# Attention with relative positions and a mixture of experts on one core: preparing the next pair's operands in other rounds and on other engines

## The reference

```python
x = x + attention(layernorm(x)); x = x + experts(layernorm(x))
# attention:
Q, K, V = x @ Wq.T + bq, x @ Wk.T + bk, x @ Wv.T + bv          # 16 heads of 8
rel_pos = arange(L)[None, :] - arange(L)[:, None] + 127        # rows of relative_k, relative_v; clipped
scores = einsum('bhld,bhrd->bhlr', Q, K) / sqrt(8) + einsum('bhld,lrd->bhlr', Q, relative_k[rel_pos])
attn = softmax(scores)
out = einsum('bhlr,bhrd->bhld', attn, V) + einsum('bhlr,lrd->bhld', attn, relative_v[rel_pos])
return out @ Wo.T + bo
```

## Time and profile before

| what | value |
|---|---|
| median of 3 runs | 2184.48 us (2182.93 to 2188.32) |
| profiled execution, its own time | 2185.62 us |
| its span | 2183.6 us |
| mean granted TensorE clock | 0.992 |
| TensorE busy | 2092.8 us, 96% of the span |
| VectorE busy | 1704.3 us, 78% |
| ScalarE busy | 1502.6 us, 69% |
| GpSimd busy | 1059.9 us, 49% |

### The profile page before, as it was taken

The page is one execution under the profiler, slowest core; times in us unless marked ns, Lnnn a source line. Parts: engine busy times, 40 slices in busy tenths (PEclk is TensorE's granted clock), DMA queues, the critical chain, the costliest instruction groups (busy, mean ns, idle before and its releaser), DMA issues.

```text
span 2183.6 us, 88119 instructions
## 1 busy us (share of the span) xinstructions
PE 2092.8 (96%) x37442; PEld 1546.1 (71%) x37442; DVE 1704.3 (78%) x3959; ACT 1502.6 (69%) x3290; POOL 1059.9 (49%) x992
## 2 busy tenths in 40 slices
PE   3999999999999999999999999999998999999998
PEld 2776777777677767777776777677776777777776
DVE  4888888888788888888887888888875666667675
ACT  3666676666666666766666666666665888888887
POOL 2444343344344443443443444434423777777676
PEclk8999999999999999999999999999999999999999
DMA  5112211321221122113212211222112112212210
GB/s 137 41 45 66 73 54 44 84 64 54 65 73 52 46 65 72 54 45 84 63 54 65 73 50 47 65 63 64 44 54 32 27 23 24 27 21 24 29 20 11
DMA packets 255679, 114.46 MB, mean 52 GB/s; under 512 B 142218, under 2 KB 251156, under 8 KB 255348
## 3 DMA queue, kind: packets, MB, share of 16 engines
q1 hardware_dynamic: 255348, 109.60, 20.4%
HBM read 83.34 MB, written 8.39 MB: 42 GB/s over the span
## 4 chain that ended last, share of the span: by engine, by line
PE 74%; DVE 9%; ACT 7%; issue 4%; POOL 3%; SPq 1%; DMA 1%; ACTq 0%; POOLq 0%; DVEq 0%
PE ps L1253 17%; PE ps L1186 10%; PE ps L1273 9%; PE ps L1283 7%; PE ps L1193 7%; PE ps L1204 6%; POOL probs_t L498 3%; DVE probs_t L791 2%; ACT probs L643 2%; ACT probs L576 2%; PE ps L1434 2%; PE ps L1417 2%; PE ps L1419 2%; PE ps L1418 2%; PE ps L1435 2%
## 5 line engine op out<-in xcount | busy, mean ns | idle before, releaser
L576 ACT ACTIVATE probs<-ps,neg_max 128x512 f32<-128x512 f32 x1024 | 690.4, 686 | 396.0 <-DVE neg_max L786 396.0
L786 DVE TENSOR_REDUCE neg_max<-ps 128x1 f32<-128x512 f32 x1024 | 635.5, 683 | 123.6 <-PE ps L1193 120.9
L437 POOL TENSOR_TENSOR stat_hi<-q_twice,mask8h 128x1024 f16<-128x1024 f16 x128 | 243.8, 1904 | 851.6 <-PE ps L1193 739.2
L1253 PE MATMUL ps<-const,probs 128*128 128x128 f32 x4096 | 506.1, 275 | 21.5 <-DVE probs_t L791 20.2
L1253 PEld LDWEIGHTS ps<-const,probs 128*128 128x128 f32 x4096 | 454.0, 142 | 62.4 <-issue 26.8
L791 DVE COPY probs_t<-ps 128x512 f32<-128x512 f32 x512 | 339.3, 682 | 91.4 <-PE ps L1253 89.5
L498 POOL TENSOR_TENSOR probs_t<-probs,probs_t 128x1024 f16<-128x1024 f32 x160 | 340.0, 2133 | 109.3 <-ACT probs_t L649 109.3
L566 ACT ACTIVATE probs_t<-ps 128x512 f32<-128x512 f32 x512 | 283.9, 596 | 149.1 <-PE ps L1253 145.0
L1186 PE MATMUL ps<-keys,stat_hi 128*32 128x512 f16 x4096 | 318.0, 383 | 0.0
L1193 PE MATMUL ps<-rk_split,stat_rel 96*32 96x512 f16 (+2 forms) x4096 | 281.5, 340 | 0.0
L995 DVE SCALAR_TENSOR_TENSOR keys<-ps,comb,keys 128x128 f32<-128x128 f32 x640 | 179.8, 344 | 129.2 <-PE ps L1436 129.2
(11 more groups left out here) (136 smaller groups left out, 2859.4 us busy)
## 6 DMA issues: line engine op xcount, KB each, us to landing
rv_step<-in_rv_win SPq DMA_DIRECT2D x128, 512.0 KB, 3.8
keys<-keys SPq DMA_DIRECT2D x64, 96.0 KB, 2.4
x_pair<-in_x SPq DMA_DIRECT2D x8, 512.0 KB, 4.3
q_twice<-q_hi SPq DMA_DIRECT2D x32, 128.0 KB, 3.0
q_lo_pair<-q_lo SPq DMA_DIRECT2D x32, 128.0 KB, 2.5
rel_scratch<-rel_t SPq DMA_DIRECT2D x256, 16.0 KB, 3.2
x_pair<-in_x SPq DMA_DIRECT2D x16, 256.0 KB, 3.1
x_pair<-rel_scratch SPq DMA_DIRECT2D x64, 64.0 KB, 4.0
```

The source lines that it names most:

```text
L576: nc.scalar.activation(probs[:, q, :], ps[:, i, :], ACT.Exp, bias=neg_max[:, q:q + 1], accum_out=row_sum[parity][:, s * QUADS + q:s * QUAD ...
L786: nc.vector.tensor_reduce(neg_max[:, q:q + 1], ps[:, i, :], op=ALU.max, axis=AX_X, negate=True).then_inc(max_done, 1)
L1253: last = nc.tensor.transpose(ps[:, bank, rt * P:(rt + 1) * P], probs[:, q, rt * P:(rt + 1) * P], ident)
```

## The change

- GpSimd takes over four kinds of work from VectorE: `normalised` (eight instructions behind `deviations`, after the spreads of step 8), `low_queries` and the low third of `q_split` (`split_low`, after the spreads of steps 14 and 15), and `v_far` (`far_values`, after the spreads of step 2, now from `v_s` and not from PSUM).
- VectorE does its statistics two tiles at a time in the rounds (2, 1) to (5, 1), the aggregation of each two tiles one step later ((3, 1) to (6, 1)), the variances at the end of (6, 1).
- `low_keys` goes from the ends of (10, 1) and (11, 0) to (11, 0) and (12, 0), straight behind the maxima; the two halves of `split_queries` that VectorE keeps go from the ends of (12, 1) and (13, 0) to (13, 0) and (14, 0), behind the maxima as well. `reduce_values` stands ahead of `values`.
- The relative piece becomes four pieces of eight transposes, in bank 1 alone, in (13, 1), (14, 0), (14, 1) and (15, 0); ScalarE copies all four. The transposed probabilities always use the banks 0, 4, 5, 6.
- queries, natural: from (11, 0), (11, 1), (12, 0), (12, 1) to (11, 1), (12, 1) for the queries and (12, 0), (13, 0) for natural.
- SyncE's copies of the keys are issued in steps 11 and 12, one sequence each, in place of both in step 11.
- Semaphores are split to match; the first pair's preparation follows the same division of work.

The core of the diff (renamed semaphores and the first pair's calls left out):

```diff
-AHEAD = {(8, 0): "rows0", (8, 1): "rows1", (9, 0): "keys0", (9, 1): "keys1", (11, 0): "queries0", (11, 1): "queries1",
-         (12, 0): "natural0", (12, 1): "natural1", (14, 1): "relative0", (15, 0): "relative1"}
+AHEAD = {(8, 0): "rows0", (8, 1): "rows1", (9, 0): "keys0", (9, 1): "keys1", (11, 1): "queries0", (12, 0): "natural0",
+         (12, 1): "queries1", (13, 0): "natural1", (13, 1): "relative00", (14, 0): "relative01", (14, 1): "relative10",
+         (15, 0): "relative11"}
...
+            def normalised(pair):
+                pool.wait_ge(rstd_ready, START + pair + 1)
+                for t in range(8):
+                    nc.gpsimd.tensor_scalar(x_pair[:, t, :], x_pair[:, t, :], mv[:, t, 0:1], rstd[:, t:t + 1],
+                                            ALU.subtract, ALU.mult).then_inc(xn_ready, 1)
+            def low_queries(pair, b):
+                pool.wait_ge(hi_ready, START + pair * 4 + 2 + b + 1)
+                nc.gpsimd.tensor_tensor(q_lo[:, cols], q_f[:, cols], q_hi[:, cols], ALU.subtract).then_inc(q_low_ready, 1)
+            def split_low(pair, b):
+                pool.wait_ge(q_split_ready, START + pair * 2 + b + 1)
+                nc.gpsimd.tensor_tensor(q_split[:, b, :, 2, :, :], natural, q_split[:, b, :, 0, :, :], ALU.subtract).then_inc(q_split_low, 1)
+            def far_values(pair, b):
+                pool.wait_ge(v_ready, START + pair * 2 + b + 1)
+                nc.gpsimd.tensor_tensor(v_far[:, b, :, :], v_s[:, b * RT + FAR:b * RT + RT, :], ..., ALU.add).then_inc(v_far_ready, 1)
...
                     spread_relative(s)
-                    if ahead and s == 7:
+                    if s == 2:
+                        for b in range(2):
+                            far_values(pair, b)
+                    if ahead and s == 8:
                         deviations(pair + 1)
+                        normalised(pair + 1)
+                    if ahead and s == 14:
+                        split_low(pair + 1, 0)
+                    if ahead and s == 15:
+                        for b in range(2):
+                            low_queries(pair + 1, b)
+                        split_low(pair + 1, 1)
...
-            def relative_queries(pair, b, bank, first):
+            def relative_queries(pair, b, half, bank, first):
                 if not first:
                     act.wait_ge(stat_ready, START + pair * STEPS * STAT_OPS)
-                act.wait_ge(q_rel_tr, START + pair * 4 + b * 2 + 1)
+                act.wait_ge(q_rel_tr, START + pair * 4 + b * 2 + half + 1)
...
+                if ahead and (s, j) in ((11, 0), (12, 0)):
+                    low_keys(pair + 1, 1 - parity, s - 11)
+                if ahead and (s, j) in ((13, 0), (14, 0)):
+                    split_queries(pair + 1, s - 13)
+                if j == 1 and products:
+                    reduce_values(*trailing)
```

More of the change, by code:

```diff
@@ L352, in pair_windows @@
                         store_rel(pair - 1, row_before, STEPS + s - 3)
-                    if ahead and s == 11:
-                        for b in range(2):
-                            copy_keys(pair + 1, 1 - parity, b)
+                    if ahead and s in (11, 12):
+                        copy_keys(pair + 1, 1 - parity, s - 11)
                     if ahead and s == STEPS - 2:
@@ L830, in score_round @@
                         values(pair, b, PIECE_BANK)
-                    if piece == f"relative{b}":
-                        relative_queries(pair + 1, b, 0, False)
-                trailing = (pair, s - 2) if s >= 2 else (pair - 1, STEPS + s - 2)
-                products = s >= 2 or not first
                 if j == 0:
@@ L839, in score_round @@
                     if transposed:
[L840 removed]
+                        evacuate(*before, IN_ROUND)
                     if products:
@@ L1044, in setup @@
                 dve.wait_ge(setup_pool, SETUP_POOL)
-            statistics(0, 0)
-            statistics(0, 1)
+            for n in range(4):
+                statistics(0, n)
+                if n:
+                    aggregates(0, n - 1)
+            aggregates(0, 3)
             variances(0)
-            normalised(0, 0)
-            normalised(0, 1)
             setup()
@@ L1226, in evacuated, with transposes @@
                 pe.wait_ge(evac_dve if q % IN_ROUND < 2 else evac_act, START + done)
-            def transposes(pair, s, j, first, piece, here=None):
+            def transposes(pair, s, j, first, here=None):
                 pe.wait_ge(exp_done, START + pair * TILES + s * QUADS + IN_ROUND * (j + 1))
                 for q in range(IN_ROUND * j, IN_ROUND * (j + 1)):
-                    bank = tr_bank(q, piece)
+                    bank = tr_bank(q)
                     if bank == TR_BANKS[0]:
@@ L1241, in transposes @@
                         last_q = TR_BANKS.index(bank)
-                        if q % IN_ROUND == 3 and tr_bank(0, piece) == bank:
-                            evacuated(pair, s, IN_ROUND * j)
-                        elif j:
+                        if j:
                             evacuated(pair, s, last_q)
@@ L1316, in score_round @@
                         natural_queries(pair + 1, b, PIECE_BANK)
-                    if piece == f"relative{b}":
-                        relative_queries(pair + 1, b, 0)
+                    for half in range(2):
+                        if piece == f"relative{b}{half}":
+                            relative_queries(pair + 1, b, half, PIECE_BANK)
                 here = (pair, s, j, first, ahead)
@@ L1469, in _ @@
                 natural_queries(0, b, 6 + b)
-            relative_queries(0, 0, 0)
+            for half in range(2):
+                relative_queries(0, 0, half, half)
             pe.wait_ge(k_ready, START + 2)
-            relative_queries(0, 1, 2)
+            for half in range(2):
+                relative_queries(0, 1, half, 2 + half)
             pe.wait_ge(q_rel_ready, START + 4)
```

192 lines of the change are left out of this document (89 added, 103 removed).

## The result

The changed kernel takes 2174.95 us (median of 5 runs, 2172.2 to 2177.57) against 2184.48 us (2182.93 to 2188.32). The ratio is 0.9951, with a 95% interval of 0.9935 to 0.9967: 9.5 us faster, where the forecast was 21.2. The profiled execution took 2177.57 us with a span of 2175.8, against 2185.62 and 2183.6 before, so between the two traces there are 7.8 us to be told.

A forecast was written before the change was run, and what follows sets the result against it. The prediction took TensorE, busy for 96% of the span, to bound the kernel. Its terms, -8.0 - 8.2 - 6.6 + 1.6 = -21.2 us, gave 2163 us, with an 8-in-10 range of 2147 to 2177.

The forecast's parts named there:

- own values: Rounds (0, 1) and (1, 0): VectorE's copy out of bank 0 comes sooner; 1.0 us in each of eight pairs, 8.0 us gained.
- statistics, normalising: Rounds (6, 1) to (8, 0): VectorE's maxima no longer late; 1.2 us in each of seven pairs, 8.2 us gained.
- keys, queries, natural: Rounds (11, 0) to (13, 0): k_lo no longer held by GpSimd's spread; 0.95 us in each of seven pairs, 6.6 us gained.
- relative queries without the clock: Rounds (13, 1) to (15, 0): bank 0 waits go, a new ScalarE wait comes; 0.2 us per pair, 1.6 us lost in seven.
- the hold: In (13, 1) ScalarE's first relative copy waits for step 15's spreads; round 9.2 us instead of 6.6, costing 2.6 us.
- start: Start of the kernel: slower normalising on GpSimd may be offset by VectorE's set-up; taken as 0, 1.1 us either side.
- eight normalisings at 0.40: GpSimd's normalising, sized from a 399 ns row: 3.2 us for eight, against VectorE's 0.27 each; up to 1.1 us at kernel start.
- The other end of the bound: GpSimd's normalising at the power's rate of 0.2 us per column: 26 us for one instruction.
- Rival 1: ScalarE's wait in (13, 1) is met early or hidden: 18 us less, 2145 us; chance 0.09.
- Rival 2: bn_aggr, at the ends of four second rounds, contends with GpSimd as k_lo did: 14 us, time 2177; chance 0.10.
- Rival 3: ScalarE bounds the relative rounds; (14, 0) to (15, 0) take 7.1 us each, not 6.5: 13 us, time 2176; chance 0.09.
- Rival 4: GpSimd's normalising is slower; TensorE waits in (9, 0) beyond 1.85 us each; at 3.0 us each, time 2227; chance 0.06.

The follow-up runs named there:

- e_nohold: Changed kernel with step 15's last 8 query rows kept in a small tile, so ScalarE's first relative copy no longer waits for GpSimd's spreads: 2149.49 us.
- e_warm_half: Changed kernel, wait kept, with TensorE transposing the identity 10 times into a free bank during the wait in (13, 1): 2166.38 us.
- e_norm_dve: e_nohold with the preparing pairs' normalising back on VectorE, four instructions each at the ends of (7, 1) and (8, 0): 2159.88 us.
- e_best: Changed kernel without the wait in (13, 1), and with the first pair's normalising, low queries and low thirds of q_split back on VectorE: 2144.06 us.

## Why the prediction was half right

The terms, as forecast and as summed over the pairs from the two traces:

| term | forecast, us | measured, us |
|---|---|---|
| own values | -8.0 | -7.8 |
| statistics, normalising | -8.2 | -8.2 |
| keys, queries, natural | -6.6 | -6.7 |
| relative queries without the clock | +1.6 | +0.9 |
| clock after the hold | not in the sum | +7.5 |
| start | 0 (up to 1.1) | +4.5 |
| end of the last pair | not in the sum | +2.3 |
| (3, 1) of the last pair | not in the sum | -0.35 |
| sum | -21.2 | -7.8 |

**The step that failed** is in the part on relative queries: "The new wait thus costs 2.6 us". It charged the wait with its own length. The hold itself was right to 0.1 us in five pairs (9.19 us) and to 0.15 in two, and the last two of the four rounds as well, at 6.59 and 6.48 us. But TensorE, which had been busy throughout, stood still for 1.86 to 2.42 us, and came back at half its clock for 3.4 us in five of seven pairs, about 1.5 us each. Three things show that it is this: the granted clock of 0.51 in the fourth pair's stretch, e_nohold, which has neither, and e_warm_half, which keeps the hold and half fills the pause. The trace of before had one pause of this length inside the pairs, in (3, 1) of the last one, where TensorE waits for a transfer, and behind it the clock stayed at 1.00; TensorE and the stretch behind the pause:

```profile
1493.22 0.65 PE L1283 MATMUL ps<-probs_t,rv_step 128*32 128x128 f32 x16 [2.50 <-DMA rv_step<-in_rv_win]
```

```profile
1493.22:1496.62 3.40, 3.40 (x57) 2.51 (x61) 1.57 (x3) 1.09 (x2) 1.96 (x2) 1.00 0.00 0
```

Ahead of the experts it had one of 4.27 us, and from 1651.9 to 1662.1 us the clock was at 0.50. So its rows spoke for either outcome, and I should have asked what the idle time that was forecast does to the engine that idles. The Trainium skill, TensorE: Matmul & The Clock Gate, section "HAM oscillation — how this bites in real kernels", tells of waits between bursts of matmuls after which each burst begins at half clock. This trace agrees in five of seven pairs, with waits shorter than those of the page, and that rule belonged among the rivals.

**The term that was mis-sized** is the start, "eight normalisings at 0.40". They took 7.04 us together, 0.80 us each but for the first, which ran beside an instruction of VectorE and took 1.59; in the other pairs all took 0.80. The nearest row was a product of float16 numbers with 128 columns, half as long; this one is float32 with two operands per row. The other end of the bound, 26 us each, was far off. In the pairs the longer time cost TensorE nothing: in the fourth the eight take 6.25 us, up to the spreads of step 9, and (6, 1) to (8, 0) are busy throughout. At the start nothing hides it. The range of 1.1 us on this term came from the same wrong number. That the low weights would come to stand between the first spreads was not seen at all. The Trainium skill, GPSIMD Engine Reference, section "Performance versus the Vector engine", has GpSimd at about twice VectorE's time; here it is 797 ns against VectorE's 339, 2.35 times, and 1154 ns against 692 for the low queries, 1.7 times. The 0.54 us that followed from it in the prediction was nearer than my row, and still low. VectorE's normalising in the kernel before, the line's nanoseconds:

```profile
L739 DVE TENSOR_SCALAR x_pair<-x_pair,mv,rstd x64: 330/339/1320, 12.1 to 1340.1; 128x128 f32<-128x128 f32 x64
```

**The cause behind a term that was right.** The statistics and normalising came out at -8.2 us as forecast, but the prediction put their 1.2 us per pair down to VectorE's work alone. The 2.08 us row shown with e_norm_dve says that a part was VectorE waiting for GpSimd's spread in (7, 1), about 1 us in each of seven pairs. How the 8.2 us divide between the statistics and the normalising was not tried. In the own values the 1.0 us per pair holds for six of the eight; the first pair gave 0.33 and the last 1.23.

**The end** is from executions and not from the change. In the changed kernel's trace a transfer came late ahead of the experts and the clock was low afterwards; TensorE and the stretch behind it:

```profile
1659.13 0.66 PE L1381 MATMUL ps<-const,x_pair 128*128 128x128 f32 x4 [1.99 <-DMA x_pair<-rel_scratch]
```

```profile
1659.90:1663.30 3.40, 3.40 (x15) 2.19 (x15) 1.38 (x2) 0.59 (x1) 0.33 (x1) 0.50 0.00 0
```

From the last round to the end it took 553.6 us, against 551.3 before; in other kernels with the same end it took 550.9 (e_nohold, e_norm_dve) or 553.2 (e_best). Over all ten traces it is the same transfer: where TensorE waits 1.86 to 2.17 us for it, the clock falls and the end takes 552.9 to 553.7 us (four traces); where it waits 1.46 to 1.81 us, the clock stays and the end takes 550.9 to 551.5 us (six).

**The rivals.** Rival 1 is false: ScalarE is held in every pair. Rival 2 is false: no aggregation took over 180 ns. Rival 3 is false: (14, 1) and (15, 0) take 6.59 and 6.48 us. Rival 4 is false: 0.8 us is far below the 1.85 from which it would decide. The time came out near rivals 2 and 3, for neither of their reasons, which is chance. What the forecast said of low keys held: k_lo never took more than 752 ns, after 2199 at most before.

What decides in a given pair whether the clock falls stays open. In the ten traces, from 60 us to the first matmuls of the experts (about 1700 us), TensorE makes 49 pauses of 1.0 to 1.81 us, and the clock falls behind none of them; of 31 pauses of 1.86 to 2.78 us it falls behind 20, and behind all ten of 4.3 us. Pauses of the same 2.41 us are found on both sides.

## What to carry to other kernels

When a change makes a steadily busy TensorE wait, charge the wait twice: its own length, and what may run slowly after it. Here no pause of up to 1.81 us cost more than itself, and 20 of the 31 pauses of 1.86 to 2.78 us did. The 2.6 us of this hold became 3.7 on average, and copying 8 rows aside to avoid the wait was worth 26 us in seven pairs. Work that is free on an idle engine in the steady state is paid in full at the start, so write the first pair's preparation for the fastest engine; and a stretch of TensorE at half clock looks fully busy, so look at the granted clock and at the count of instructions in it.

## What the runs showed of the hardware

- A pause of TensorE of 1.86 to 2.42 us let the granted clock fall to half for 3.4 us in five of seven pairs of the changed kernel. Ten transposes of 128x128 in it, 1.26 us of work, kept the clock at 1.00 in seven of seven.
- VectorE's normalising, with one matrix and two numbers per row from SBUF, was held until the end of a GpSimd spread: 2.72 us for four against 1.11. bn_stats (at most 285 ns) and bn_aggr (at most 180 ns) were not held beside the same spreads.
- A large subtraction on VectorE (128x2560, two inputs from SBUF) and GpSimd's spreads ran one after the other when they met, whichever came first. In the changed kernel the spread ends at 42.78 us, the subtraction 2.68 us later at 45.46 (2.82 us alone), and the four small spreads behind it 1.34 us later at 46.80 (1.47 alone), though they are shown as running from 40.95 and 42.75.
